# Softmax sums of two key tiles from one ones product, the first tile added to the second by a DMA

## What is computed

```python
p = jax.nn.softmax(qk / sqrt(512), axis=-1)
p = p * jnp.triu(ones((s, s)))
z = einsum('bhqk,bhkd->bhqd', p, v)
x = layernorm(embedded + z) * gamma + beta
```

## Time and profile before

| what | value |
|---|---|
| median of three runs | 1189.59 us |
| span of the profiled execution | 1187.2 us |
| one batch, start to start of attention | 140.8 us |
| PE busy | 1149.0 us (97%) |
| DVE, ACT, POOL busy | 784.1, 492.9, 401.8 us |
| DMA moved | 111.71 MB, mean 94 GB/s |

### The profile page before, as it was taken

The page is one execution under the profiler, slowest core; times in us unless marked ns, Lnnn a source line. Parts: engine busy times, 40 slices in busy tenths (PEclk is TensorE's granted clock), DMA queues, the critical chain, the costliest instruction groups (busy, mean ns, idle before and its releaser), DMA issues.

```text
span 1187.2 us, 18377 instructions
## 1 busy us (share of the span) xinstructions
PE 1149.0 (97%) x7311; PEld 809.2 (68%) x7311; DVE 784.1 (66%) x1276; ACT 492.9 (42%) x660; POOL 401.8 (34%) x373
## 2 busy tenths in 40 slices
PE   6499999999999999999999999999999999999997
PEld 3255778667785777757777577866778577775886
DVE  5986773778737776487755777377873777648513
ACT  4475312762138511574117631276213751156311
POOL 1343423144222632235222352315332262212432
PEclk8589999999999999999999999999999999999999
DMA  8971332422224422323244133242222432232000
GB/s 303 338 208 59 112 82 56 108 97 82 73 55 109 142 69 53 87 67 141 72 91 108 55 120 78 55 108 105 74 73 56 109 142 71 48 69 68 1 1 18
DMA packets 44954, 111.71 MB, mean 94 GB/s; under 512 B 8000, under 2 KB 19648, under 8 KB 44864
## 3 DMA queue, kind: packets, MB, share of 16 engines
q1 hardware_dynamic: 40016, 98.01, 29.2%
q10 hardware_dynamic: 4848, 12.47, 3.1%
HBM read 88.95 MB, written 21.50 MB: 93 GB/s over the span
## 4 chain that ended last, share of the span: by engine, by line
PE 93%; DVE 4%; DMA 1%; ACT 1%; issue 1%; POOL 0%; SPq 0%; POOLq 0%; ACTq 0%
PE PS L1244 54%; PE PS L1156 11%; PE PS L1180 7%; PE PS L1120 6%; PE PS L1063 5%; PE PS L1187 3%; PE PS L1193 2%; DVE neg_max L784 2%; PE PS L1080 2%; DMA stacks<-qk_rows 1%; ACT probsT L678 1%; PE PS L1209 1%; PE PS L1344 1%; DMA qk_rows<-qk_lo 0%; PE PS L1288 0%
## 5 line engine op out<-in xcount | busy, mean ns | idle before, releaser
L777 DVE TENSOR_REDUCE neg_max<-PS 128x3 f32<-128x1536 f32 (+1 forms) x168 | 256.9, 1574 | 61.9 <-PE PS L1120 61.9
L540 POOL TENSOR_TENSOR hidA_lo<-hidA_full,hidA_hi 128x512 fp32r<-128x512 f32 x128 | 174.1, 1360 | 225.6 <-DVE hidA_hi L1024 180.5
L678 ACT ACTIVATE probsT<-PS 128x1024 f32<-128x1024 f32 x192 | 184.6, 1023 | 53.4 <-PE PS L1156 49.3
L1244 PE MATMUL PS<-hidA_hi,g 128*128 128x512 f32 x512 | 205.5, 401 | 0.4 <-POOL hidA_lo L540 0.4
L1244 PE MATMUL PS<-hidC_hi,g 128*128 128x512 f32 x512 | 203.0, 397 | 0.0
L1244 PE MATMUL PS<-hidA_lo,g 128*128 128x512 f32 x512 | 199.9, 391 | 0.0
L1244 PE MATMUL PS<-hidC_lo,g 128*128 128x512 f32 x512 | 199.7, 390 | 0.0
L540 POOL TENSOR_TENSOR hidC_lo<-hidC_full,hidC_hi 128x512 fp32r<-128x512 f32 x64 | 82.2, 1285 | 202.0 <-DVE hidC_hi L1024 202.0
L1156 PE MATMUL PS<-stacks 66*128 66x512 f32 x512 | 147.3, 418 | 1.6 <-DVE neg_max L784 1.1
L699 ACT ACTIVATE hidC_full<-PS,scales 128x512 f32<-128x512 f32 x64 | 44.2, 690 | 243.1 <-PE PS L1244 243.1
L699 ACT ACTIVATE hidA_full<-PS,scales 128x512 f32<-128x512 f32 x64 | 44.1, 689 | 218.6 <-PE PS L1244 218.6
(11 more groups left out here) (131 smaller groups left out, 1650.4 us busy)
## 6 DMA issues: line engine op xcount, KB each, us to landing
stacks<-qk_rows SPq DMA_DIRECT2D x124, 256.0 KB
stacks<-qk_rows SPq DMA_DIRECT2D x246, 128.0 KB
qk_rows<-qk_hi SPq DMA_DIRECT2D x16, 512.0 KB, 2.7
qk_rows<-qk_lo SPq DMA_DIRECT2D x16, 512.0 KB, 2.9
xT_sb<-xT_dram SPq DMA_DIRECT2D x8, 512.0 KB, 4.0
g_raw<-h1T_dram ACTq DMA_DIRECT2D x4, 1024.0 KB, 12.1
g_raw<-h2T_dram ACTq DMA_DIRECT2D x4, 1024.0 KB, 16.7
x_tok<-x_dram SPq DMA_DIRECT2D x8, 512.0 KB, 5.0
```

The lines of the kernel that those rows point to most:

```text
L540: nc.gpsimd.tensor_tensor(lo[:, m, :], full[:, m, :], hi[:, m, :], ALU.subtract).then_inc(lo_done, 1)
L678: nc.scalar.activation(probs(s)[:, 2 * pair:2 * pair + 2, :], PS[:, bank:bank + 2, :], ACT.Exp, scale=SCALE).then_inc(exp_done, 1)
L777: ins = nc.vector.tensor_reduce(NEGM[:, half, at:at + hi - lo], PS[:, bank:bank + hi - lo, :], AX.X, ALU.max, negate=True)
L1244: ins = nc.tensor.matmul(out, d if swapped else w, w if swapped else d, start=(k == 0 and part == 0), stop=(k == kts - 1 and part == 1))
```

## The change

After the mask of key tile 1 of a group, GpSimd issues a DMA that adds the probabilities of key tile 0, queries 128 to 511 of all four heads, onto those of key tile 1 in SBUF. The ones product of tile 0 shrinks to queries 0 to 127, that of tile 1 goes away, and at key tile 3 one ones product over the summed tile brings the denominators of both. The diagonal product of tile 1 moves into the value step of tile 2. Waits follow: value step 4g+3 on TensorE waits for the DMA; so does the exponential of step 4g+6 on ScalarE, which overwrites tile 0; the exponentials of steps 4g+3 wait for a later value step; the masks of steps 4g+1 wait for one value step more. The scratch space of DMA descriptors grows from 1024 to 2048.

```diff
--- before.py
+++ after.py
@@ -194,6 +194,7 @@
         probs_ready = sem("probs_ready")
         diag_ready = sem("diag_ready")
         pv_done = sem("pv_done")
+        sums_carried = [sem("sums_carried0"), sem("sums_carried1")]
         zT_taken = sem("zT_taken")
         rec_done, z_taken = sem("rec_done"), sem("z_taken")
         rstd_done, rstd_last_done = sem("rstd_done"), sem("rstd_last_done")
@@ -293,6 +294,15 @@
             if s == 0:
                 return PT[:, RING_C - 1, 0, :].rearrange("p (j q) -> p j q", j=QUAD)
             return PM[:, s % 4, :, :]
+
+
+        def after_carry(engine, b, g):
+
+            after(engine, sums_carried[g % 2], b, 16 * NQUAD // 2, 16 * (g // 2 + 1))
+
+        def masked_free(s):
+
+            return max(s - (2 if s % QT == 1 else 3), 0)
 
 
         CHUNKS = 2 * HT + 2 * 2 * HT + QT * 4
@@ -550,10 +560,17 @@
                     after(pool, probs_ready, b, STEPS, s + 1)
                 if not first or s >= QT + LAG:
                     return
-                after(pool, pv_done, b, STEPS, max(s - 3, 0))
+                after(pool, pv_done, b, STEPS, masked_free(s))
                 nc.gpsimd.tensor_tensor(masked(s), probs(s)[:, :, kt * P:(kt + 1) * P],
                                         MASK[:].rearrange("p (a m) -> p a m", a=1).to_broadcast([P, QUAD, P]),
                                         ALU.mult).then_inc(diag_ready, 1)
+
+            def carry_sums(b, g):
+
+                s = QT * g + 1
+                after(pool, diag_ready, b, STEPS, s + 1)
+                pool.dma_start(probs(s)[:, :, P:S], probs(s - 1)[:, :, P:S],
+                               accum_op=ALU.add).then_inc(sums_carried[g % 2], 16)
 
             def split_qk(b, parts):
                 for n in parts:
@@ -586,6 +603,8 @@
                     masks(b, s, first, bounded)
                     if s == 1 and not first:
                         rstd_last(b - 1)
+                    if s % QT == 1:
+                        carry_sums(b, s // QT)
                     if s in X_AT:
                         t = X_AT.index(s)
                         after(pool, x_in, b, 16, 16)
@@ -673,7 +692,9 @@
                     for pair in range(2):
                         after(act, scoredT, b, 2 * STEPS, 2 * s + pair + 1)
                         if s >= RING_C - 1:
-                            after(act, pv_done, b, STEPS, max(s - RING, 0) + 1)
+                            after(act, pv_done, b, STEPS, max(s - 3, 1) if s % QT == 3 else max(s - RING, 0) + 1)
+                        if s >= RING and s % QT == 2:
+                            after_carry(act, b, s // QT - 1)
                         bank = bank_T(2 * s + pair)
                         nc.scalar.activation(probs(s)[:, 2 * pair:2 * pair + 2, :],
                                              PS[:, bank:bank + 2, :], ACT.Exp,
@@ -829,7 +850,7 @@
                     after(dve, y_done, b, QT, 0)
                 after(dve, exp_done, b, 2 * STEPS, 2 * s + 2)
                 after(dve, probs_ready, b, STEPS, s + 1)
-                after(dve, pv_done, b, STEPS, max(s - 3, 0))
+                after(dve, pv_done, b, STEPS, masked_free(s))
                 nc.vector.tensor_tensor(masked(s), probs(s)[:, :, kt * P:(kt + 1) * P],
                                         MASK[:].rearrange("p (a m) -> p a m", a=1).to_broadcast([P, QUAD, P]),
                                         ALU.mult).then_inc(diag_ready, 1)
@@ -1174,25 +1195,42 @@
                         after(pe, zT_taken, b, NQUAD, g - 1)
                 after(pe, diag_ready, b, STEPS, s + 1)
                 after(pe, v_ready, b, 1, 1)
-                lo, hi = kt * P, (kt + 1) * P
-
-                for j in range(QUAD):
-                    nc.tensor.matmul(PS[32 * j:32 * j + 32, bank, lo:S], ONE[:, 0:32],
-                                     probs(s)[:, j, lo:S], start=(kt == 0), stop=False,
-                                     skip_group_check=True)
-
-                if kt:
+
+                def sums(step, tokens):
                     for j in range(QUAD):
-                        h = g * QUAD + j
-                        nc.tensor.matmul(PS[32 * j:32 * j + 32, bank, 0:lo], VXT[:, kt * VX + VW * h:kt * VX + VW * h + 32],
-                                         probs(s)[:, j, 0:lo], start=False, stop=False,
-                                         skip_group_check=True)
-
-                for j in range(QUAD):
-                    h = g * QUAD + j
-                    ins = nc.tensor.matmul(PS[32 * j:32 * j + HD, bank, lo:hi], VXT[:, kt * VX + VW * h:kt * VX + VW * h + HD],
-                                           masked(s)[:, j, :], start=False, stop=(kt == QT - 1),
-                                           skip_group_check=True)
+                        nc.tensor.matmul(PS[32 * j:32 * j + 32, bank, tokens], ONE[:, 0:32], probs(step)[:, j, tokens],
+                                         start=(step % QT == 0), stop=False, skip_group_check=True)
+
+                def below_diagonal():
+                    for j in range(QUAD):
+                        at = kt * VX + VW * (g * QUAD + j)
+                        ins = nc.tensor.matmul(PS[32 * j:32 * j + 32, bank, 0:kt * P], VXT[:, at:at + 32],
+                                               probs(s)[:, j, 0:kt * P], start=False, stop=False, skip_group_check=True)
+                    return ins
+
+                def diagonal(step):
+                    n = step % QT
+                    for j in range(QUAD):
+                        at = n * VX + VW * (g * QUAD + j)
+                        ins = nc.tensor.matmul(PS[32 * j:32 * j + HD, bank, n * P:(n + 1) * P], VXT[:, at:at + HD],
+                                               masked(step)[:, j, :], start=False, stop=(n == QT - 1),
+                                               skip_group_check=True)
+                    return ins
+
+                if kt == 0:
+                    sums(s, slice(0, P))
+                    ins = diagonal(s)
+                elif kt == 1:
+                    ins = below_diagonal()
+                else:
+                    sums(s, slice(kt * P, S))
+                    below_diagonal()
+                    if kt == 2:
+                        diagonal(s - 1)
+                    else:
+                        after_carry(pe, b, g)
+                        sums(s - 2, slice(P, S))
+                    ins = diagonal(s)
                 ins.then_inc(pv_done, 1)
 
             def turn_x2(b, part, last):
@@ -1429,7 +1467,7 @@
         "ident": np.eye(P, dtype=np.float32),
     }
     nc = bacc.Bacc("TRN2", target_bir_lowering=False, num_devices=1,
-                   dynamic_dma_scratch_size=1024)
+                   dynamic_dma_scratch_size=2048)
     args = {name: nc.dram_tensor(name + "_dram", shape, F32, kind="ExternalInput").ap()
             for name, shape in _INS.items()}
     args["out"] = nc.dram_tensor("out_dram", (B * S, D), F32, kind="ExternalOutput").ap()
```

## The result

| | before | after |
|---|---|---|
| median of four runs each, same comparison | 1189.48 us | 1277.47 us |
| ratio, 95% interval | 1 | 1.0738 (1.0723 to 1.0754) |
| span of the profiled execution | 1187.2 us | 1276.0 us |

88 us slower. The forecast was 29 us slower, with a range up to 1260: the sign held, the size did not.

A forecast was written before the change was run, and what follows sets the result against it. TensorE was taken to bound attention, VectorE close behind. Per batch 2.65 us for group 0 plus 1.5 for the clock, 4.15, over seven batches 29; 1189.6 + 29 = about 1219 us, range 1181 to 1260.

The forecast's parts named there:

- Removed from TensorE: Ones products in attention: 384 columns fewer per group, 0.65 us each time, upper bound 20.8 us.
- What of it reaches the path: Attention, no transfer late: 0.3 us won in group 0 and 1.65 in groups 1 to 3, 2.0 us per batch.
- Waits that change hands: New conditions on exponentials and masks in attention cost nothing while TensorE is not late; four extra semaphore waits not priced.
- Added: the carry: GpSimd's accumulating transfer of probabilities per group: 8 us to landing in group 0, 4.8 us in the others.
- the rival in time: First carry lands within 5.35 us of issue, so the kernel gets faster, typically 1180 us; chance 0.19.
- Group 0, where it decides: Value step 3 waits for the first carry; break-even landing 5.35 us, at 8 us the batch loses 2.65 us.
- The clock: TensorE's idle time before value step 3 may bring half speed: 1.5 us per batch, bounds 0 and 3.5.
- The other groups: Groups 1 to 3: margins of 6.4, 4.9 and 5.8 us just fit a 4.8 us carry, cost zero.
- Batch 0, "even": First batch, with masks on GpSimd and partly at half clock, counted as neither gain nor loss.
- The rule on the port between VectorE and GpSimd: Two-port VectorE operations block GpSimd's descriptor writes; normalizations beside the first carry's issue, up to 11 us, outside the sum.
- every carry is late: Rival: carries cost 8 us even on empty queues, so other groups wait too; 1242 to 1270 us; chance 0.25.

The follow-up runs named there:

- the loads held back: Only group 0 of each batch carried, and SyncE holds group 2's stack loads, x and the output store until the carry landed; 1238.0 us, ratio 1.0423.
- the kernel without a carry: Kernel after the change with the accumulating DMA and all waits for it removed, sums lacking key tile 0; 1190.66 us, ratio 1.0012.
- The plain copy: Kernel after the change with the accumulating DMA replaced by a plain transfer of key tile 1 onto itself, all waits kept; 1252.97 us, ratio 1.0528.
- Groups 2 and 3 alone: Kernel after the change, but groups 0 and 1 computed as before and only 2 and 3 carried; 1202.8 us, ratio 1.0113.
- group 0 alone: Kernel after the change, but only group 0 of each batch carried, groups 1 to 3 computed as before; 1255.04 us, ratio 1.0555.
- the kernel with groups 1 to 3: Kernel after the change, but group 0 of each batch computed as before and only groups 1 to 3 carried; 1242.44 us, ratio 1.0433.
- the gap filled in group 0 alone: Only group 0 carried, plus fourteen 512-column products into a free PSUM bank ahead of its wait, batch 0 excepted; 1235.98 us, ratio 1.0402.

## Why the prediction was wrong in size, step by step

- **"Removed from TensorE"**, 20.8 us at most: right as a count, 20.6 us of work less.
- **"What of it reaches the path"**, 2.0 us per batch: **failed.** Without any transfer it is 0.4 in the batches in which the clock holds. I weighed TensorE against VectorE's 8.20 us per group and gave 0.1 back. The waits that bind are ScalarE's exponentials behind a value step of 0.22 us, and the tail of norms that only the last scores can bring forward. Being busy 33.94 of 34 us made TensorE the bound, but by a hair, with ScalarE at 26.5 and VectorE at 26.1 in bursts that the shorter steps no longer covered.
- **"Waits that change hands"**, nothing: not so. With the diagonal product and the wait of its mask put back, the kernel without a carry takes 6.6 us less, some 3 by the pace of the batches and the rest by the clock. The move of the product had no price of its own in the sum.
- **"Added: the carry"**: 8 us in group 0 against 8.7 to 10.6 in the batches behind the first; right in kind, and the crowded stretch is what makes it so (6.9 with the loads held back). 4.8 us for the others, "nearer to the doubled read": **failed**, 6.7 to 7.2 in the medians. The plain copy at 4.0 us lies within my 3.3 to 5.1; the accumulating one lies outside. The Trainium skill's sum ("DMA: Bandwidth & Descriptors", "Anatomy of one DMA — SWDGE (gpsimd) path"), 3.8 us as an estimate, agrees with the plain copy (4.0) and not with the accumulating one. The store's rate that the rival in time rests on is 480 KB in 1.2 us, some 410 GB/s and not 430; no term of the sum hangs on it.
- **"Group 0, where it decides"**: the stall is there, 4.39 us against 4.6 foreseen, 5.2 in the mean of the eight batches. That GpSimd doesn't issue the second carry before the first has landed was in no step.
- **"The clock"**, 1.5 us per batch with bounds of 0 and 3.5: **failed**, and it is the largest miss. 111.5 us more of work at half clock is 55.8 us, some 7 us per batch, twice the upper bound. I let the clock come back with value step 3 and three score pairs; it stayed at half for 13.6 to 20.5 us, with TensorE busy for most of it. The earlier trace rows had shown a full microsecond of busy TensorE at 0.50 and I read it as the end of a recovery.
- **"The other groups"**, zero: **failed.** Groups 2 and 3 alone cost 14 us. The margin was about 5.9 us (6.67 less the 0.72 of waiting), better than my 4.9, but a carry needs more.
- **Batch 0, "even"**: 12.8 us late. Its first carry took 13.36 us.
- The rule on the port between VectorE and GpSimd, kept out of the sum, was worth little: the four normalizations beside the first carry's issue take 1.69 us in the batch shown, 1.38 before, and the issue takes 1.33 us beside them and 1.30 where VectorE stands idle.

The nearest rival was "every carry is late", at 1242 to 1270. It had the mechanism on empty queues. That its upper end, 11.5 us per batch, is near to the 10.9 measured from one feed-forward to the next is luck: 1.5 of it were for the clock, where 7 stand, and it counted a gain from the removed columns that isn't there.

What stays open: what makes the clock fall after 2.02 us of waiting in one batch and not in another, and what lets it rise. Why the second carry waits for the first, for space of descriptors or something else, wasn't tried. No version with a carry beat the kernel before.

## What to carry to other kernels

Before columns are taken off the busiest engine, ask which engine the next scores or products will run into at the finest step, not in the group's mean; here 20.6 us of work was worth nothing as the change has it, and 5 at best, in a kernel that leaves the sum over key tile 0 out. A transfer on the path of TensorE is to be priced twice: its lateness, and the clock behind it, which in these runs cost about as much again (49 to 56 us beside 49 in the kernel after, 31 beside 39 with group 0 alone). An accumulating DMA is to be measured by itself before a plain copy's duration is taken for it.

## What the runs showed of the hardware

- An accumulating SBUF to SBUF transfer of 768 KB takes 6.6 to 7.7 us from issue to landing on queues that are otherwise empty and 8.7 to 10.6 beside loads (13.4 in the first batch, 13.0 at most in the kernel with groups 1 to 3), a plain copy 4.0; GpSimd is held 1.3 us by the issue of one and 0.8 by the other.
- The granted clock fell after short waits, and in the batches shown a fully busy TensorE did not bring it back for ten microseconds and more. The length of the wait alone does not decide: with the gap filled in group 0 alone, 2.02 us were followed by full clock in one batch and by half clock in another. The shortest wait was in the kernel without a carry, where the clock fell twice behind the first batch, at 939 us and, behind a wait of 2.19 us, at 1093 (busy time by stretch for the first; the idle time before is 0.3 us, and gaps of 0.2 us in other batches were followed by full clock):

```profile
938.00:939.00 1.00, 0.74 (x3) 0.30 (x2) 0.93 (x3) 1.00 (x3) 0.00 (x0) 1.00 0.00 0
939.00:943.00 4.00, 4.00 (x46) 2.37 (x50) 3.42 (x10) 2.70 (x3) 2.10 (x3) 0.57 0.02 4
```

- A GpSimd addition of 128 x 1536 elements lasts 3.5 us and holds a VectorE mask operation (two SBUF inputs) that starts beside it to about its end, 3.3 us in place of 0.7, and the four output normalizations (one input tensor) likewise, 4.5 us in place of 1.4. A transpose out of PSUM beside it takes its usual 0.70 us.
